# Windowed attention in a hybrid kernel: the next chunk's q, k and v made between the score units

## The reference

```
qkv = _norm(x) @ W_qkv + b_qkv                 # 256 -> 3 x 256, 16 heads of 16
att = einsum('bhqd,bhkd->bhqk', q, k) / 4
allowed = (diff >= 0) & (diff < 64)            # diff = query - key
att = softmax(where(allowed, att, -inf))
y = einsum('bhqk,bhkd->bhqd', att, v)
out = x + y @ W_proj + b_proj
```

## Time and profile before

| | |
|---|---|
| median of 3 runs | 2673.03 us (2670.06 to 2679.05) |
| profiled execution, its time | 2670.67 us |
| its span, first to last instruction | 2668.9 us |
| granted TensorE clock, mean | 0.956 |
| busy: PE, DVE, ACT, POOL | 2247.7, 1968.9, 1856.0, 1549.8 us |
| attention, first DMA issue to last | 1982.8 to 2549.3 us of the span |

### The profile page before, as it was taken

The page is one execution under the profiler, slowest core; times in us unless marked ns, Lnnn a source line. Parts: engine busy times, 40 slices in busy tenths (PEclk is TensorE's granted clock), DMA queues, the critical chain, the costliest instruction groups (busy, mean ns, idle before and its releaser), DMA issues. The chain is left out here.

```text
span 2668.9 us, 40685 instructions
## 1 busy us (share of the span) xinstructions
PE 2247.7 (84%) x14744; PEld 1351.1 (51%) x14744; DVE 1968.9 (74%) x2761; ACT 1856.0 (70%) x3169; POOL 1549.8 (58%) x1342
## 2 busy tenths in 40 slices
PE   0789898898998998988989989863659899988867
PEld 0345455454454554554545545532436666666644
DVE  3389889888898888898888988875635555555544
ACT  0598988888989989889899898862614433343452
POOL 1189889898898898898988988991100000000010
PEclk9899999999999999999999999985789999999989
DMA  5413404314234244042241340405020000000031
GB/s 180 103 33 87 100 26 114 85 35 112 57 71 117 66 99 99 21 119 66 55 111 41 88 99 24 116 1 180 1 102 1 17 17 17 17 17 17 17 113 63
DMA packets 125980, 180.54 MB, mean 68 GB/s; under 512 B 11218, under 2 KB 74194, under 8 KB 125396
## 3 DMA queue, kind: packets, MB, share of 16 engines
q1 hardware_dynamic: 125780, 177.94, 24.7%
HBM read 135.43 MB, written 42.47 MB: 67 GB/s over the span
## 5 line engine op out<-in xcount | busy, mean ns | idle before, releaser
L617 POOL TENSOR_TENSOR h<-h,C_rep 128x512 f32<-128x512 f32 x1024 | 1275.6, 1283 | 197.2 <-ACT h_carry L536 197.2
L423 DVE TENSOR_TENSOR_SCAN h<-decay,h_carry,psum 128x512 f32<-128x512 f32 x768 | 955.4, 1269 | 126.4 <-PE psum L745 95.4
L528 ACT ACTIVATE decay<-dt_rep,A 128x512 f32<-128x512 f32 x1024 | 729.4, 713 | 99.2 <-DVE h L423 92.2
L745 PEld LDWEIGHTS psum<-ident,u_B 128*128 128x128 f32 x4096 | 476.2, 141 | 559.2 <-DVE h L423 309.4
L745 PE MATMUL psum<-ident,u_B 128*128 128x128 f32 x4096 | 629.9, 280 | 140.1 <-DVE h L423 108.2
L548 ACT ACTIVATE u_B<-u_tok,B_tok 128x512 f32<-128x512 f32 x832 | 589.3, 710 | 63.9 <-PE psum L745 45.8
L423 DVE TENSOR_TENSOR_SCAN h<-decay,zero,psum 128x512 f32<-128x512 f32 x256 | 318.8, 1270 | 52.1 <-PE psum L745 34.7
L1412 POOL TENSOR_TENSOR a_rstd<-a_vareps,a_minushalf 128x4 f32<-128x4 f32 x9 | 9.2, 1017 | 502.9 <-DVE a_vareps L1442 502.9
L754 PE MATMUL psum<-h,state_sum 128*32 128x512 f32 x2048 | 279.7, 619 | 11.3 <-POOL h L617 10.9
L1564 ACT ACTIVATE a_probs<-a_probs 128x512 f32<-128x512 f32 x128 | 80.6, 630 | 257.6 <-DVE a_probs L1502 257.6
L606 POOL TENSOR_TENSOR u_B<-u_tok,B_tok 128x512 f32<-128x512 f32 x192 | 200.9, 1046 | 42.9 <-DVE u_tok L395 42.9
(11 more groups left out here) (201 smaller groups left out, 2826.0 us busy)
## 6 DMA issues: line engine op xcount, KB each, us to landing
dt_rep<-dt_rows SPq DMA_DIRECT2D x256, 256.0 KB, 5.5
C_rep<-C_rows SPq DMA_DIRECT2D x256, 64.0 KB, 2.0
dt_rows<-x_dt_gated SPq DMA_DIRECT2D x16, 1024.0 KB, 4.8
x_tok<-mamba_residual SPq DMA_DIRECT2D x16, 512.0 KB
residual<-mamba_residual SPq DMA_DIRECT2D x16, 512.0 KB, 3.9
mamba_residual<-residual SPq DMA_DIRECT2D x16, 512.0 KB, 2.9
a_x<-after_slots SPq DMA_DIRECT2D x9, 512.0 KB, 5.2
f_gru_weights<-in_slot_gru_dram SPq DMA_DIRECT2D x2, 2176.0 KB
```

Source lines behind the costliest of these rows:

```text
L423: dve.tensor_tensor_scan(h[:, slot(u)], dec[:, u % DEC], PS[:, u % 2], first, ALU.mult, ALU.add)\
L528: act.activation(dec[:, u % DEC], dtr[:, k % EG], ACT.Exp, scale=A[:, s // STEPS, k:k + 1]).then_inc(S["decay"], 1)
L617: pool.tensor_tensor(h[:, slot(u)], h[:, slot(u)], crep[:, k // EG], ALU.mult).then_inc(S["hc"], 1)
L745: ins = pe.transpose(PS[:, u % 2, tb * P:(tb + 1) * P], pr[:, f % 2, tb, eg], ident[:])
```

## The change

`attention` is written anew, with one loop over all 128 units n of all chunks (and 6 steps of drain). Step n issues scores(n), values(n-3), transp(n-2); the rings of `a_probs` and `a_probs_T` are one buffer longer (4 and 3). In units 7 to 14 of each chunk, one of eight steps `prepare(s, m)` of the next chunk stands behind the unit on PE: two of transposes, two of q, two of k, two of v. All use one PSUM bank, 7, and step m waits until step m-1 has been copied out. ACT copies out transposes, q and k (one copy each), DVE adds v's bias.

q is copied out once, as it is (`a_q`), and SP copies 16 rows of it for each head into `a_q_by_head` with DMAs from on-chip memory to on-chip memory, 16 a chunk. The rest of `a_q_by_head` was set to zero once, at the start, for both buffers. v is multiplied once (`a_v_tile`); GpSimd makes the version shifted by 64 tokens (`a_v_skewed`) with three copies. The keys before the chunk are copied from the last chunk's k and not multiplied again. Keys, q by head and v have two buffers. The normalisation's last step moves from DVE to GpSimd. Output goes out by tile (128 KB), not by chunk (512 KB).

In the diff, `by_head` is SP's, `v_skew` GpSimd's, and the loops at its end are PE's.

```diff
-        xnT = sb("xn_feat", [P, KT, WIN + C])
-        qS = sb("q_by_head", [P, NH, C])
-        V = sb("v", [P, 2, TG, NH, HW + 1])
-        pr = sb("probs", [P, 3, 4, P])
-        pT = sb("probs_T", [P, 2, 4, P])
+        xnT = sb("xn_feat", [P, KT, C])
+        qF = sb("q", [P, KT, C])
+        qS = sb("q_by_head", [P, 2, NH, C])
+        V1 = sb("v_tile", [P, 2, TG, NH, HW + 1])
+        V0 = sb("v_skewed", [P, 2, TG, NH, HW + 1])
+        pr = sb("probs", [P, 4, 4, P])
+        pT = sb("probs_T", [P, 3, 4, P])
...
+    STATS, AGGR, PREP, FIN, YT, PROJ, ADD = 0, 4, 7, 7, 8, 9, 10
...
+                def by_head(s):
+                    if s >= 2:
+                        sp.wait_ge(S["s_mm"], (s - 1) * U)
...
+                    for h in range(NH):
+                        if h % FH == 0:
+                            sp.wait_ge(S["q"], KT * s + h // FH + 1)
+                        rows = slice(h % FH * HW, (h % FH + 1) * HW)
+                        sp.dma_start(qS[rows, s % 2, h], qF[rows, h // FH]).then_inc(S["qS"], 16)
...
+                def v_skew(s):
...
+                    pool.tensor_copy(V0[0:WIN, k], V1[0:WIN, k]).then_inc(S["v0"], 1)
+                    pool.wait_ge(S["v0"], 3 * s + 1)
+                    pool.tensor_copy(V0[WIN:P, k, 0:1], V1[WIN:P, 1 - k, TG - 1:TG]).then_inc(S["v0"], 1)
+                    pool.wait_ge(S["v0"], 3 * s + 2)
+                    pool.tensor_copy(V0[WIN:P, k, 1:TG], V1[WIN:P, k, 0:TG - 1]).then_inc(S["v0"], 1)
...
-                    for u in range(U + 2):
-                        if u < U:
-                            scores(u)
-                        if u >= 2:
-                            values(u - 2)
-                        if 1 <= u <= U:
-                            transp(u - 1)
...
-                    features(s + 1)
-                    ytr(TG - 1)
-                    project(TG - 1)
+                for m in range(8):
+                    prepare(0, m)
+                for n in range(LAST + 1):
+                    if n < NU:
+                        scores(n)
+                    if 3 <= n < NU + 3:
+                        values(n - 3)
+                    if 2 <= n < NU + 2:
+                        transp(n - 2)
...
+                    s, m = chunk_at(n, PREP)
+                    if s and 0 <= m < 8:
+                        prepare(s, m)
```

More of the change, by code:

```diff
@@ L1318 @@
 A_BK = A_BQ + KT
-A_HM = A_BK + KT
-A_BV = A_HM + FH
-A_BP = A_BV + D
+A_BV = A_BK + KT
+A_BP = A_BV + 2 * D
 A_ALL = A_BP + D
@@ L1369, in attention, with tile_at, chunk_at @@
         ld = [signals.add(f"a_x_loaded{k}") for k in range(2)]
[L1370 to L1378, removed]
+        stored = [signals.add(f"a_stored{k}") for k in range(8)]
+        def tile_at(n, lag):
+            J, rest = divmod(n - lag, HG)
+            return J if rest == 0 and 0 <= J < NJ else None
+        def chunk_at(n, at):
+            s, u = divmod(n, U)
+            return (s + 1, u - at) if s + 1 < N and n < NU else (None, None)
         with nc.Block() as block:
@@ L1403, in _ @@
+                for k in range(8):
+                    sp.wait_ge(stored[k], 16 * NJ // 8)
             @block.gpsimd
@@ new lines, in add @@
+                def add(J):
+                    dve.wait_ge(S["o_mm"], J + 1)
+                    dve.wait_ge(S["xb"], J // TG + 1)
+                    if J >= 8:
+                        dve.wait_ge(stored[J % 8], 16 * (J // 8))
+                    dve.tensor_tensor(yo[:, J % 8], PS[:, 6, D:2 * D], xb[:, J // TG % 2, J % TG], ALU.add).then_inc(S["o"], 1)
+                for i in range(TG):
+                    stats(0, i)
+                variance(0)
+                dve.memset(qS[:, 0], 0.0).then_inc(S["zero"], 1)
@@ new lines, in transp, with values @@
+                def transp(n):
+                    pe.wait_ge(S["exp"], n + 1)
+                    if n >= 2:
+                        pe.wait_ge(S["pT"], n - 1)
+                    for i in range(4):
+                        ins = pe.transpose(PS[:, 2 + n % 2, i * P:(i + 1) * P], pr[:, n % 4, i], ident[:])
+                    ins.then_inc(S["p_tp"], 1)
+                def values(n):
+                    s, u = divmod(n, U)
+                    j, r = divmod(u, HG)
+                    J = s * TG + j
+                    pe.wait_ge(S["pT"], n + 1)
+                    if u == 0:
+                        pe.wait_ge(S["v0"], 3 * (s + 1))
+                    if r == 0 and J >= 2:
+                        pe.wait_ge(S["y"], J - 1)
+                    for i in range(4):
+                        h = 4 * r + i
+                        for blk in range(2):
+                            ins = pe.matmul(PS[WIN * blk:WIN * (blk + 1), 4 + J % 2, h * (HW + 1):(h + 1) * (HW + 1)],
+                                            pT[:, n % 3, i, WIN * blk:WIN * (blk + 1)], (V1 if blk else V0)[:, s % 2, j, h],
+                                            start=True, stop=True)
+                    ins.then_inc(S["av"], 1)
```

504 lines of the change are left out of this document (246 added, 258 removed).

## The result

The changed kernel takes 2552.2 us (median of 4 runs, 2550.06 to 2555.78). Before, in the same comparison, took 2674.71 (2670.06 to 2679.05). The ratio is 0.9544 (95% interval 0.9523 to 0.9564): 122.5 us faster. The forecast was 2561 with a range of 2546 to 2606. Direction and size came out as said, and so did what bounds the kernel now: PE, with a full list. The period, the prologue and the last chunk were mis-sized, and the reason given for the units' waits, too short a lead, is not the one that the runs show.

A forecast was written before the change was run, and what follows sets the result against it. PE was taken to bound the kernel, though not full (busy 40.90 of 46.35 us in the units). Savings of 103.5 + 3.7 + 5 = 112.2 us from 2670.67 gave 2558.5, plus 2.4 to the runs' median: 2561 us, range 2546 to 2606.

The forecast's parts named there:

- The period: One chunk's work as one PE list without a tail: 53.4 us instead of 68.2, saving 103.5 us over seven periods.
- the prologue: First chunk, before its first scores: two q/k steps at half clock, scores at 2015.3 instead of 2019.0, saving 3.7 us.
- the last chunk: From the last chunk's first mask to its last addition, 53.00 us before: saves 5 us (3 to 8).
- the units' waits: Attention units: each loses 0.48 us, 7.7 a chunk, from one unit of lead; one unit more removes it.
- The waits for the hand-over of the steps: PE's gaps at the operand change after each of eight prepare steps: 0.16 us each, 1.3 a chunk.
- the lower clock: Between the units of two chunks: granted clock 0.92, PE falling to 1.2 GHz behind the tail's waits.
- The q copies: SP's 16 on-chip copies a chunk: 0.42 us each plus 2.0 to land, 8.7 us, hidden under 23 us.
- Normalisation on GpSimd: Before step 7's token transposes: root 1.02 us and four operations of 0.6, 3.4 us, hidden in a 6.5 us window.
- rival B: GpSimd late: at 2.35 us an operation step 7's transposes wait 3.9 us a chunk, total 2588 us; chance 0.06.
- A: Rival: the units keep their pace of 2.74 us, period 61.1, total 2622 us; chance 0.14.
- C: Rival: q copies don't overlap, 32 us against 23, PE waits 9 a chunk, total 2624 us; chance 0.04.
- D: Rival, better than forecast: no gaps between steps and a warm prologue, total 2546 us; chance 0.06.

The follow-up runs named there:

- the best kernel: The changed kernel with the first chunk's prepare steps in separate banks, its normalisation on DVE, and four of its 16 q copies issued by ACT: 2538.7 us.

## Why the prediction was right, and where it was not

**The period** (forecast 53.4, measured 51.56, below the lower bound of 52.1). The sum of PE's list, 52.1, was right to 0.5 us: v, the transposes of the tiles and those of the tokens are each 0.1 shorter, the 16 units 0.2. The waits for the hand-over of the steps, 1.3 a chunk, did not exist. 7 x 1.84 = 12.9 us more than forecast are this. Another 4.0 us is a term that I had left out: the first chunk's list holds no values, transposes and tile ends of units before it, hence 47.60.

**Its parts.** Here the reason failed, not the sum. By the runs, of 68.2 us ACT's order takes away 6.5 (61.64 left; 4.5 of it waits, 2.0 clock), the second v 3.5, and 6.6 are the rest. Of these 0.8 is the k of the 64 tokens before (2147.92 to 2148.76 in before), and 4.4 are PE's idle time with the order turned, of which all but one wait of 0.61 lie in the first units of a chunk and in its tail; what is left was not taken apart. The prediction had 7.7 for the units' waits, where 4.5 were, and said that one more unit of lead on each consumer removed them. ACT's order was part of the change, but got no price. And it put the lower clock down to the tail's waits; but with ACT's order turned and the tail still there, the clock stays at 1.00. The trace of before held the answer, in a view that the prediction did not read: ACT's own timeline, where the copy stands right behind an exp that had waited 1.27 us for DVE.

**The q copies**: hidden, as said; no wait of the scores on them. The term was too low, since an on-chip copy of 16 rows takes SP 0.59 us (median) rather than 0.42:

```profile
L1402 SPq DMA_DIRECT2D a_q_by_head<-a_q x128: 512/589/1431, 2005.8 to 2367.3; - x128
...
DMA to landing us min/median/max: 1.9/2.0/3.1
```

**Normalisation on GpSimd**: just hidden, with luck in the size. An operation took 1.22 us, twice the 0.6 assumed:

```profile
L1435 POOL TENSOR_SCALAR a_xn<-a_x,a_meanvar,a_rstd 128x256 f32<-128x256 f32 x32 | 38.7, 1221 | 0.8
...
L1459 POOL COPY a_v_skewed<-a_v_tile 64x1088 f32<-64x1088 f32 x8 | 8.7, 1082 | 211.6 <-DVE a_v_tile L1498 211.6
```

The root and four of them are 5.9 of the 6.5 us of the window; in one chunk, row by row:

```profile
2136.17 4.83 POOL L1435 TENSOR_SCALAR a_xn<-a_x,a_meanvar,a_rstd 128x256 f32<-128x256 f32 x4
...
2141.67 0.60 PE L1630 MATMUL a_psum<-a_ident,a_xn 128*128 128x128 f32 x4
```

They end at 2141.00, 0.67 us before PE wants them. The 1.3 us an operation from which rival B would have begun was missed by 0.1, by luck. All 32 operations took 1217 to 1237 ns, so DVE's work beside them held none of them up.

**The prologue** (forecast 3.7, measured 0.05). From the first issue to the first mask 32.5 us were forecast (2015.3 less 1982.8), and 36.15 measured. Most of the 3.65 between is the clock.

```profile
1986.18 0.36 SPq L1388 DMA_DIRECT2D a_x<-after_slots  x1
...
1993.25 4.85 POOL L1435 TENSOR_SCALAR a_xn<-a_x,a_meanvar,a_rstd 128x256 f32<-128x256 f32 x4
...
2001.18 3.78 PE L1635 MATMUL a_psum<-a_xn_feat,a_weights 128*128 128x512 f32 x4 [0.69 <-ACT a_xn_feat L1563]
...
2005.74 3.78 PE L1635 MATMUL a_psum<-a_xn_feat,a_weights 128*128 128x512 f32 x4 [0.78 <-ACT a_q L1569]
...
2010.30 3.78 PE L1635 MATMUL a_psum<-a_xn_feat,a_weights 128*128 128x512 f32 x4 [0.78 <-ACT a_q L1569]
...
2014.86 1.98 PE L1635 MATMUL a_psum<-a_xn_feat,a_weights 128*128 128x512 f32 x4 [0.78 <-ACT a_k L1580]
```

q's first step starts 15.0 us after the first issue, where the forecast had 14.5. Two errors cancel there: GpSimd's four operations take 4.85 us rather than 2.4, and x landed sooner, DVE's statistics starting 3.8 us after its issue where it had been 5.7. From there to the first mask it is 21.15 us rather than 18.0. Three steps of q and k ran at the lower level, 1.2 GHz (3.78 us, against 1.98 for the fourth), not two, and that is 2.0 us; the rest is 0.1 to 0.3 in each step. The eight matmuls of q and k (16 records) took 13.3 us of PE, where they take 7.03 in a later chunk. With the banks apart they took 10.00, and 8.60 in the best kernel, at granted clocks of 0.82 and 0.88 up to the first mask rather than 0.69. The Trainium skill (TensorE: Matmul & The Clock Gate, "What you observe") says that sustained activity releases the clock; the trace agrees: the gaps of 0.7 to 0.8 us between the steps went, and PE spent 3.3 to 4.7 us less on the same matmuls.

**The last chunk** (5, measured 3.2): the waits of the units were worth less than the 7.7 that stand in its sum, 4.5 at full clock and 6.5 with the clock, and the rest was not taken apart. The 1.2 us at the end of the stage were not counted.

**Rivals.** A fell (no wait of the units is left). B did not come; its threshold, 1.3 us an operation, is still only worked out. C did not come, and the number of transfers from which PE waits is now measured. D, 2546, was nearer to the result than 2561: its "no gaps" came, its warm prologue did not (with other banks it came in part). Of the signs named, three were narrowly or clearly missed though the forecast held: masks 53 to 54 us apart (51.56), the first mask by 2022 (2022.33), the copies issued within 10 us (10.05 and 10.82 in the two chunks read).

## What to carry to other kernels

For each wait of the full engine, read the timeline of the engine that it waits for: if the awaited instruction stands behind one that itself waits for something later, exchange the two before adding buffers. Short waits can cost twice, in time and in clock: read the granted clock period by period, in both kernels. Where one engine can be made full, its list summed from rows without waits is the forecast, and the rest of the work is to show that each other chain fits its window; for transfers compare the number issued, times the issue time, with the window. A prologue with hand-overs in one bank pays for them twice, in the gaps and in the clock.

## What the runs showed of the hardware

GpSimd took 1.22 us for a subtract-and-multiply by two per-row values on 256 columns, three times DVE's 0.40, though its copy of 1088 columns on 64 rows takes 1.08. An on-chip copy of 16 rows costs SP 0.59 us to issue and lands in 2.0 us, many at a time. PE fed without a gap kept full clock for 345 us. It fell to the lower level in the last units of a chunk of before, behind waits of 1.44 and 0.69 us, and ahead of the first mask where it had stood still for 2.60 and 3.01 us; behind the 1.13 us of the last kernel it did not.
